# ScalarE's normalization and predicated copies in the opening, and other ends of the edge stages, in one graph-and-experts kernel

## The reference, cut to what matters

```python
x = x + gnn(_layernorm(x), stack([src, dst]), ...)      # L = 2 layers
x = x + experts(_layernorm(x)[None], ...)[0]
# one layer of gnn:
h = x @ w_in + b_in                                     # before the first layer
xn = _layernorm(h, ln1_g[l], ln1_b[l])
q, k, v = xn @ wq[l] + bq[l], xn @ wk[l] + bk[l], xn @ wv[l] + bv[l]   # 8 heads of 32
scores = einsum('ehd,ehd->eh', q[dst], k[src]) * scale  # dst, src: the edges and every node's edge to itself
attn = softmax of scores over the edges of each dst
agg = segment_sum(attn[:, :, None] * v[src], dst)
h = h + agg.reshape(n, 256) @ wo[l] + bo[l]
h = h + gelu(_layernorm(h, ln2_g[l], ln2_b[l]) @ w1[l] + b1[l]) @ w2[l] + b2[l]
```

## Time and profile before

| | us |
|---|---|
| median of 3 runs | 3311.08 (3309.96 to 3312.67) |
| the profiled execution, device time | 3308.49 |
| its span | 3306.3 |
| opening, to the first edge gather | 0 to 199.5 |
| edges(0), first to last gather issue | 199.5 to 1306.2 |
| tail of edges(0), links, mid | 1306.2 to 1690.4 |
| edges(1), first to last gather issue | 1690.4 to 2790.0 |
| tail of edges(1) to the end | 2790.0 to 3306.3 |

### The profile page before, as it was taken

How to read it: one execution, slowest core, us unless ns; L and a number is a source line. 1 busy time by engine, 2 the same in 40 slices (tenths; PEclk the granted TensorE clock), 3 DMA queues, 4 the chain that set the end, 5 groups by cost and what they waited for, 6 DMA issues and landing times. The chain is left out here.

```text
span 3306.3 us, 28610 instructions
## 1 busy us (share of the span) xinstructions
PE 2235.3 (68%) x7207; PEld 1510.9 (46%) x7207; DVE 2490.4 (75%) x3966; ACT 1320.9 (40%) x3886; POOL 1834.8 (55%) x1938
## 2 busy tenths in 40 slices
PE   6745666656566666699956665666666666699798
PEld 4423443433343343476643333344433433477676
DVE  6788888888888888545448888888888888455233
ACT  2224444445545444211224444554544544222222
POOL 5047777777777776212047777777777775221000
PEclk8866767677777766799976777777677767699899
DMA  5357777777777778323357777777777777332111
GB/s 145 105 169 236 243 243 243 243 243 243 245 246 246 243 243 244 84 62 86 82 162 236 244 243 243 243 245 245 246 246 243 244 243 234 78 79 55 45 32 39
DMA packets 249750, 623.51 MB, mean 189 GB/s; under 512 B 50258, under 2 KB 105777, under 8 KB 249592
## 3 DMA queue, kind: packets, MB, share of 16 engines
q0 software_dynamic: 149904, 471.38, 47.9%
q1 hardware_dynamic: 99688, 150.30, 14.6%
HBM read 526.66 MB, written 94.78 MB: 188 GB/s over the span
## 5 line engine op out<-in xcount | busy, mean ns | idle before, releaser
L811 POOL DMA_INDIRECT ring<-kv_table,stage_ix x1760 | 1672.7, 950 | 601.6 <-issue 539.7
L1078 PE MATMUL bank<-ring,hot_w 128*128 128x272 f32 x1760 | 709.9, 543 | 516.9 <-DVE ring L2026 467.3
L1065 PE MATMUL bank<-qs,hot_q 128*128 x1760 | 691.5, 535 | 358.4 <-DVE ring L2003 295.6
L1078 PEld LDWEIGHTS bank<-ring,hot_w 128*128 128x128 f32 x1760 | 418.1, 259 | 790.9 <-DVE ring L2026 630.6
L2003 DVE TENSOR_TENSOR ring<-ring,bank 128x1024 f32<-128x1024 f32 x440 | 533.7, 1213 | 282.0 <-DMA ring<-kv_table,stage_ix 254.9
L1065 PEld LDWEIGHTS bank<-qs,hot_q 128*128 128x128 f32 x1760 | 444.6, 263 | 513.0 <-issue 423.9
L2008 DVE TENSOR_REDUCE s<-ring 128x32 f32<-128x1024 f32 x440 | 533.9, 1213 | 4.2
L1293 ACT ACTIVATE hot_q<-pos_b,row_of 128x128 f32<-128x128 bf16 x880 | 301.0, 392 | 25.2 <-DVEq L1991 16.5
L2020 DVE TENSOR_TENSOR bank<-ring,bank 128x512 f32<-128x512 f32 x440 | 301.8, 686 | 0.0
L2017 DVE TENSOR_TENSOR ring<-ring,bank 128x512 f32<-128x512 f32 x440 | 297.7, 677 | 0.0
L2026 DVE TENSOR_TENSOR ring<-ring,bank 128x512 f32<-128x512 f32 x440 | 295.9, 673 | 0.4
(11 more groups left out here) (333 smaller groups left out, 2214.8 us busy)
## 6 DMA issues: line engine op xcount, KB each, us to landing
agg_d<-stage_o SPq DMA_DIRECT2D x108, 544.0 KB, 4.4
ring<-kv_table,stage_ix POOLq DMA_INDIRECT x1760, 3.8
pos_b<-rel_d SPq DMA_DIRECT2D x54, 256.0 KB, 5.4
kv_table<-ring SPq DMA_DIRECT2D x50, 224.0 KB
h_dram<-ring SPq DMA_DIRECT2D x15, 560.0 KB
ring<-h_dram SPq DMA_DIRECT2D x15, 560.0 KB
ring<-in_x_dram SPq DMA_DIRECT2D x10, 560.0 KB
ring<-kv_table SPq DMA_DIRECT2D x10, 560.0 KB
```

Of the source, the lines that this page charges most:

```text
L811: gps.indirect_dma_start(out=chunk[:, par * G + i, j, :], out_offset=None, in_=table, in_offset=bass.IndirectOffsetOnAxis(ap=stage_ix[:, p ...
L1065: mm = ten.matmul(q_bank(third, i)[:, 0:QC], hot_q[:, i % 4, a * P:(a + 1) * P], qs[:, bass.ds(t * QC + a * QC, QC)], start=(a == 0), stop ...
L1078: mm = ten.matmul(b_acc[i % 2][:, lo - OWN:MC], hot_w[:, i % 4, :], chunk[:, s, j, lo:ROW], start=(j == 0), stop=(j == QD // 2 - 1), skip_ ...
```

## The change

The change moves the opening's norms to ScalarE (GpSimd adds -mean * rstd), does `expand` with a copy and two predicated copies, moves `constants` ahead, weighs ten blocks per layer in one product of 128x1024 with GpSimd adding the pairs, holds SP's weight loads until the last gather has landed, moves parts of `fold` into `links`, does the first batch of mid and last tile by tile, and turns every `hold` but those whose increment is read into a plain wait.

```diff
@@ SyncE
-                        hold(sp, s["done"], ...)
+                        sp.wait_ge(s["done"], ...)
                     if nn == LASTG:
+                        sp.wait_ge(gath[(NB - 1) % SLOTS], (layer + 1) * uses((NB - 1) % SLOTS) * QD * 16)
                         next_weights()
@@ GpSimd, opening: root
                     gps.tensor_scalar(r[:, :], m[:, :, 1], EPS, 1.0, ALU.add, ALU.mult).then_inc(s["rs_step"], 1)
+                    gps.tensor_scalar(f[:, :], m[:, :, 0], -1.0, 0.0, ALU.mult, ALU.add).then_inc(s["rs_step"], 1)
...
+                    gps.tensor_tensor(f[:, :], f[:, :], r[:, :], ALU.mult).then_inc(s["rs_ready"], 1)
@@ GpSimd, homes: one semaphore per tile in the first batch
-                                               in_offset=...).then_inc(s["home"], 16)
+                                               in_offset=...).then_inc(s["home"] if it else S[f"first{j}"], 16)
@@ GpSimd, after the gathers of a layer (LATE = 2)
+                def add_pairs(par, i, n):
+                    pool.wait_ge(S["weighed"], n + 1)
+                    val = chunk[:, par * G + i, :, D:ROW]
+                    gps.tensor_tensor(val[:, 0:2], val[:, 0:2], val[:, 2:4], ALU.add).then_inc(S["w_ready"], 1)
...
+                for k in range(NGRP - 2, NGRP):
+                    for i in range(LATE if k == NGRP - 2 else 0, blocks_of(k)):
+                        add_pairs(k % 2, i, layer * NB + k * G + i)
@@ TensorE
-                turn(0)
-                project(0, 0)
+                for j in range(BT + 1):
+                    if j < BT:
+                        turn_tile(0, j)
+                    if j:
+                        project_tile(0, 0, j - 1)
@@ TensorE, links: between the transposes (L1142) and the product (L1147)
+                if layer:
+                    fold_ups("last")
+                else:
+                    fold_rows("mid")
...
             links(0)
-            fold("mid")
+            fold_ups("mid")
...
             links(1)
-            fold("last")
@@ ScalarE, opening
+                def scaled(at, no, src, j0=0, j1=BT):
+                    r, f = ((rs_x, off_x), (rs, off))[no % 2]
+                    act.wait_ge(s["rs_ready"], no + 1)
+                    if at:
+                        act.wait_ge(s["evac"], at)
+                    for j in range(j0, j1):
+                        sca.activation(tok[:, j, :], src[:, j, :], ACT.Identity, bias=f[:, j:j + 1], scale=r[:, j:j + 1]).then_inc(s["tok"], 1)
+                scaled(0, 0, x_in)
                 turned(0)
+                scaled(o.first(1), 2, x_in)
                 for it in range(NBATCH):
                     if it + 1 < NBATCH:
                         turned(o.first(it + 1))
+                    scaled(o.second(it), 2 * it + 1, h_in[it % 2])
                     turned(o.second(it))
                     for j in range(BT):
                         keys(it, j)
                         if it + 1 < NBATCH:
                             query(it, j)
+                        if it + 2 < NBATCH and j >= 2:
+                            scaled(o.first(it + 2), 2 * it + 4, x_in, 2 * j - 4, min(2 * j - 2, BT))
@@ VectorE, expand
-                do(ts(e_bit, e_m, float(n), None, ALU.is_ge))
-                do(vec.scalar_tensor_tensor(out=e_m, in0=e_bit, ...))
-                to, by = e_pack[:, :, n:P, :], e_move[:, :, n:P, :]
-                do(tt(by, e_pack[:, :, 0:P - n, :], to, ALU.subtract))
+                of, to = (e_pack, e_move) if k % 2 == 0 else (e_move, e_pack)
+                st.did(vec.tensor_copy(to, of))
+                do(ts(e_bit, e_m, float(n), None, ALU.is_ge))
+                st.did(vec.scalar_tensor_tensor(out=e_m, in0=e_bit, ...))
                 for a in range(2):
-                    st.did(tt(by[:, a], by[:, a], e_bit[...].to_broadcast(...), ALU.mult))
+                    bit = e_bit[:, a, n:P].bitcast(U32).rearrange("p (e j) -> p e j", j=1).to_broadcast([HB, P - n, QD])
+                    st.did(vec.copy_predicated(to[:, a, n:P, :], bit, of[:, a, 0:P - n, :]))
                 st.sync(v)
-                do(tt(to, to, by, ALU.add))
@@ VectorE, opening: scaled, turn_x and turn_h are gone; constants() before measure_x(1)
                 projected(0)
+                constants()
                 measure_x(1)
...
-                    turn_h(it)
                     projected(it + 1)
...
-                    if it == 0:
-                        constants()
-                    if it + 2 < NBATCH:
-                        turn_x(it + 2)
-                    else:
-                        turn_h(it + 1)
@@ VectorE, edges: the steps of groups 26 and 27
+                def weigh_late(par, i, n):
+                    val = chunk[:, par * G + i, :, D:ROW].rearrange("p j (d h) -> p j d h", h=H)
+                    w = w_of[:, i].rearrange("p j (a h) -> p j a h", a=1)
+                    tt(val, val, w.to_broadcast([P, QD, DH, H]), ALU.mult).then_inc(S["weighed"], 1)
...
+                    if nn == LASTG:
+                        for i in range(LATE):
...
+                        weigh_late(par, LATE, n + LATE)
+                        weigh_late(par, LATE + 1, n + LATE + 1)
+                        scores(1 - par, LASTG - 1, tn, n + (nk + LASTG - 1), third + 1)
+                        sum_scores(1 - par, LASTG - 1, n + (nk + LASTG - 1))
+                        weigh_late(par, LATE + 2, n + LATE + 2)
+                        return
+                    if not nn:
+                        sum_weights()
+                        for i in range(nk):
+                            weigh_late(par, i, n + i)
+                        return
@@ VectorE, mid and last: the first batch, instead of head(0) and projected(0, ...)
+                def first_head(h, st):
+                    hd = Steps(s["head"])
+                    v.wait_ge(s["x_in"], 2 * ROWS)
+                    hd.did(bias(h_n[kind], bias_sq))
+                    v.wait_ge(s["out_free"], 1)
+                    def put(j):
+                        v.wait_ge(s["mm"], j + 1)
+                        tt(h[:, j, :], h_n[kind][:, j, :], bank[4 + j % 3][0:TN, 0:D], ALU.add).then_inc(s["bank_free"], 1)
+                    def stats(j):
+                        v.wait_ge(s["bank_free"], j + 4)
+                        st.did(vec.bn_stats(stat[:, j, :], h[:, j, :]))
+                    for j in range(BT):
+                        v.wait_ge(S[f"first{j}"], (1 if kind == "mid" else 2) * 16)
+                        own, z = home[:, j, 0:H], home[:, j, H:2 * H]
+                        val = home[:, j, 2 * H:MC].rearrange("p (d h) -> p d h", h=H)
+                        den = small[0:TN, j * H:(j + 1) * H]
+                        mine = own_v[:, j, :].rearrange("p (d h) -> p d h", h=H)
+                        hd.did(tt(den, z, own, ALU.add))
+                        hd.did(tt(mine, mine, own.rearrange("p (a h) -> p a h", a=1).to_broadcast([TN, DH, H]), ALU.mult)); hd.sync(v)
+                        hd.did(ts(den, den, 1e-30, None, ALU.max))
+                        hd.did(tt(mine, mine, val, ALU.add)); hd.sync(v)
+                        hd.did(vec.reciprocal(den, den)); hd.sync(v)
+                        tt(tok[:, j, :].rearrange("p (h d) -> p d h", h=H), mine, den.rearrange("p (a h) -> p a h", a=1).to_broadcast([TN, DH, H]), ALU.mult).then_inc(s["tok"], 1)
+                        if j >= 2:
+                            put(j - 2)
+                            if j >= 3:
+                                stats(j - 3)
+                    assert hd.n == HEAD0, hd.n
+                    put(BT - 2)
+                    stats(BT - 3)
+                    put(BT - 1)
+                    stats(BT - 2)
+                    stats(BT - 1)
+                    st.sync(v)
+                    aggregate()
```

More of the change, by code:

```diff
@@ L68 @@
 LANES = P - G * H
+LATE = 2
+assert LASTG == LATE + 2 and LATE + 3 == G - 3
+HEAD0 = 5 * BT + 1
 QSPACE = 7700
@@ L535, in batch @@
                 def batch(it, last):
-                    hold(sp, s["done"], it + 1, S["sp_passed"])
+                    sp.wait_ge(s["done"], it + 1)
                     tile_rows(rows(out, it), h_b, S["out_done"])
@@ L900, in fold, with fold_ups @@
                             mm = ten.matmul(b[0:TN, 0:c1 - c0], g_col[:, 1, a:a + 1].to_broadcast([P, TN]), w_qkv[:, a, c0:c1], start=(a == 0), stop=(a == 1))
-                if kind in ("mid", "last"):
-                    for f in range(FFN // P):
-                        for a in range(2):
-                            mm = ten.matmul(bank[6][:, f:f + 1], w_up[:, a, f * P:(f + 1) * P], g_col[:, 3, a:a + 1], start=(a == 0), stop=(a == 1))
+                    mm.then_inc(S["w_pe"], 1)
+            def fold_ups(kind):
+                pe.wait_ge(S["w_in_dma"], 16 * W_TOTAL[kind])
+                for f in range(FFN // P):
+                    for a in range(2):
```

(20 more changed lines are left out.)

133 lines of the change are left out of this document (67 added, 66 removed).

## The result

The changed kernel took 3266.97 us (median of 4 runs, 3265.53 to 3270.23), the kernel before 3311.07 beside it: a ratio of 0.9869, 95% interval 0.9853 to 0.9885. The prediction was 3269, so the total was right; several of its terms were not, and their errors largely cancel. The profiled span went from 3306.3 to 3264.3 us, 42.0 less.

| stretch | before | after | change | predicted |
|---|---|---|---|---|
| opening, to the first edge gather | 199.5 | 181.1 | -18.4 | -20 |
| edges(0), first to last gather issue | 1106.7 | 1106.6 | -0.1 | 0 |
| tail 0: last gather issue to the first instruction of links | 32.9 | 25.3 | -7.6 | -7.0 |
| links 0: from there to the first home gather | 19.2 | 17.2 | -1.9 | 0 |
| first batch of mid: from there to its first aggregate | 24.6 | 19.6 | -5.0 | -6 |

The account below looks back on a forecast made before the run. GpSimd's issue of gathers was taken to bound both edge stages; opening -20, tails -7.0 and -3.6, links +2.3, first batches -12 sum to -40.3 us, giving 3268 against the profile, 3271 against the median; predicted 3269, range 3254 to 3287.

Parts of the forecast that it names:

- Opening, norms, -10: Opening: ten sets of five scalings leave VectorE for ScalarE; their worth, read at three places, is -7, -1.7 and -1.3 us.
- the first, -7: Opening: the last node row issues at 72.2 instead of 76.55, so `rows_of_nodes` starts at 76.4 instead of 83.36: -7 us.
- The second place, -1.7: Opening: the set of scalings behind the tables of `rows_of_nodes` leaves VectorE: -1.7 us.
- The third, -1.3: Opening: the next x set leaves VectorE, which then waits for TensorE's queries: -1.3 us (0 to -3).
- The two sets after that I cost at nothing: Opening: two later sets of scalings give 0, as TensorE's keys pace VectorE; without that cover, 3.4 us more.
- Expand, -10: Opening, seven expands: difference and sum go, a copy comes, predicated copies cost what the products did: -10 us (-14 to +1.6).
- SP's new wait removes that: Tail of layer 0: VectorE's 3.40 us wait for the last gather, beside weight loads, goes; with the tail's -3.6: -7.0 us.
- Links 1, +2.3: Links, layer 1: 32 products (6.83 us) go ahead of L1147 in a 4.58 us gap, ending at 2832.07 instead of 2829.82.
- B: Rival, tails: GpSimd's adds pace them, at 2.1 us each; 4 us lost per layer, total 3277; chance 0.12.
- D: Rival, opening's expand: the predicated copy is no stream; 14 copies at 5 us each cost 61, total 3330; chance 0.04.
- E: Rival, whole kernel: the change shifts work without moving the ends; total within 0.2% of now; chance 0.04.
- A: Rival, opening: TensorE and ScalarE pace it; of 20 us only 9 remain, total 3280; chance 0.16.

Follow-up runs that it names:

- run 1: The changed kernel with the old expand (difference, masked product, sum) put back: 3273.34 us.
- run 3: The changed kernel without SP's wait for the last gather ahead of the weight loads: 3267.41 us.
- run 6: The changed kernel with the 32 narrow products of fold (fold_ups) behind the product of links in layer 1, as before: 3264.03 us.
- run 2: The kernel before with the new expand alone: 3300.02 us.
- run 11: The kernel before with every hold whose increment nobody reads as a plain wait, nothing else: 3304.70 us.
- run 4: The changed kernel with the ten adds of a layer back on VectorE, each behind its product: 3279.10 us.
- run 5: The changed kernel with the old first batch of mid and last (five tiles at once): 3276.02 us.
- run 12: The changed kernel with TensorE's opening reordered, node rows earlier, fold_ups behind links' product, three wide products ahead, each layer's last add on VectorE: median 3258.99 us.
- run 10: The changed kernel with fold_ups behind the product of links in layer 1 and three unread wide products in the gap ahead: 3264.67 us.

## Why the prediction was right, and which of its steps were not

- **The bound** was read rightly: the gathers' pace stayed, and every gain ahead of them moved what follows one to one. That the total came within 2 us is in part luck: by the table, the stretches miss by 4.0 us in all on one side and by 5.5 on the other.
- **Opening, norms, -10:** measured -10.2 at the first own score of batch 3 (147.63 before, 137.46 now), but by other steps. Of the prediction's three places the first, -7, gave 3.4 (83.36 to 79.99). "The first run of node rows, which does not move" failed: it started at 34.81 instead of 30.67, since the root of the second x batch ahead of it came later (31.92 instead of 29.00). Ahead of that root stand `projected(0)`, whose first tile came at 19.64 instead of 16.85, and `constants`, which was costed at nothing and now ends at 29.6, 2.9 us after VectorE had begun that batch before. The tile is late because ScalarE's scalings begin 1.2 us later than VectorE's did (12.99 and 11.82), behind GpSimd's longer root, and its evictions of the transposes stand behind all five of them (first at 15.46 instead of 13.05). The second place, -1.7, gave 1.6. The third, -1.3, gave 3.1 (from `projected(3)` to the next own score). "The two sets after that I cost at nothing" failed too: they gave 2.0 (2.8 up to `projected(4)`, 139.53 before and 128.57 now, of which 0.8 are lost again). Too much by 3.6 and too little by 3.8: the -10 is right by luck.
- **Expand, -10:** 11.9 in itself, since a copy took 0.70 and a pair of predicated copies 1.35 (taken: 0.72 and 1.28), and waits between its steps went too; net 8.3 by run 1 and 8.1 by the two traces, because "they are late next" of TensorE was right and worth 3.6 to 3.9 us, which the sum left out. The whole opening gave 18.4 in the profiled run; by the spread of the other runs it is 14 to 19.
- **Tails:** -7.6 and -5.3 where -7.0 and -3.6 were predicted. VectorE's part was right (its last product ends 9.3 and 6.9 us earlier by the last gather's issue; predicted 10.2 and 6.8). The lag behind it was too dear: 1.2 for the add and 2 for lags were taken, 1.66 was measured (3.43 us from the last product's end to links, 1.77 before), because TensorE did a block in 1.1 us, not 1.86, as it had already done in the last blocks before. A gap on ScalarE for a store of `agg_d`, a sign of being wrong, was there (1.15 us), but the last block waited for GpSimd's last add, which ended at 1311.2. "SP's new wait removes that" failed as a step: by run 3 the 3.40 us went without the wait as well, since VectorE now asks later; whether the loads caused them before stays open.
- **Links 1, +2.3:** the mechanism was right, the term mis-sized: 4.5 by run 6, while the holds' end gives some of it back. Of the 4.5, 3.0 are the held product (its gap was 3.2 to 3.8 us in runs 2, 6 and 11, not 4.58) and 1.5 the longer scatters, a term that the prediction did not have.
- **Links 0, 0:** -1.9. Of it 0.63 is the hold ahead of the home gathers; TensorE at its full level takes 1.9 off the product, of which VectorE's wait for it shows 1.2 (0.79 instead of 1.95).
- **First batches, -6 each:** -5.0 and -5.9. In mid the first home gather's issue took 2.48 us instead of 1.24 because of VectorE's addition beside it (last section), which the prediction put at nothing.
- **Holds, 0:** failed. Where nothing covers them they cost: 0.63 at each first home gather and some 1.5 in mid by run 11.
- **Rivals.** B fell by run 4 and the 1.27 us of one add, D by the 0.70 and 1.35 above, E by runs 1 and 5. A was half there: TensorE and then ScalarE do pace the opening's end, and cost some 3 to 4 us of the sum, not 11.

## What to carry to other kernels

When one engine's work in a serial opening is shortened, put a price on the engine that is late next, not only a warning: here it kept 3 to 4 us, and taking that away only showed the one behind it. Filler work moved into a gap must be shorter than the gap at the clock that the engine will have there. An operation moved into an engine's idle time can stretch what another engine does there: VectorE's addition of 1.49 us cost about 1 us of GpSimd's DMA issues in each layer. And a sum that comes out right can stand on two wrong steps: only landmarks between them, compared in both traces, show it.

## What the runs showed of the hardware that was not expected

**A scan that waits for GpSimd.** VectorE's second scan (L2127) took 1.28 us in the tail, and 0.41 in run 4, where GpSimd adds nothing; it ended 0.3 us after GpSimd's pair of adds (1299.95 + 2.53). Both its inputs lie in SBUF; the first scan and the late products, with one input in a PSUM bank, kept their 0.40 and 1.2 us beside the adds. The other way round, GpSimd's small power operation took 4.46 us beside a VectorE product of two SBUF operands, against 1.17 in most others, and the root for which ScalarE waited 8.35 us came 3.3 us later for it:

```profile
82.69 4.46 POOL L738 TENSOR_TENSOR rs_x<-rs_x,half 125x5 f32<-125x5 f32 x1
...
82.65 3.48 DVE L1529 TENSOR_TENSOR ring<-ring,qs 125x3200 f32<-125x3200 f32 x1
```

The Trainium skill says so of the two engines (GPSIMD Engine Reference, section 1): they share their SBUF interfaces, and get in each other's way where a VectorE instruction has two SBUF inputs. The trace agrees, and shows that two inputs are not the only case: a GpSimd product of 125x5 took 1.85 us instead of 0.20 beside VectorE's cast of one SBUF tensor (L740 at 80.02, L1527 at 79.99 for 1.83). The sharing would also explain why the adds paid here, the products beside them reading their weights from PSUM; no run moved the weights.

**GpSimd's DMA issues stretch in the same way.** Beside VectorE's addition of 125x1280, both operands in SBUF, an indirect DMA's issue lasted longer by the time that the two overlapped, less 0.12 or 0.13 us: overlaps of 1.36, 1.21, 1.10, 1.09 and 0.75 us (the first home gather of mid and the second scatter of links 1 in the changed kernel, the first home gather of mid in runs 6 and 12, the second in run 4) made them 1.24, 1.08, 0.98, 0.97 and 0.63 longer. Where the addition stood elsewhere, as in run 5, the same issues took 1.00 and 1.24 us.

**TensorE's clock moves the first gather by some 2.8 us** from run to run with the same program. From the end of TensorE's 6 us pause to the transposes of expand's result it took 25.1 us in the changed kernel and 25.2 in run 6, but 27.8 and 28.0 in runs 4 and 10, granted 0.50 from 164 to 168 us where the others had 1.00. Those two have the late first gathers (184.8 and 185.2; the others 180.6 to 182.4); the last 1 us of their delay arose ahead of that pause. What decides between the levels there is not shown. In links, behind narrow products as behind a pause, the product took 3.95 and 3.97 us; behind wide ones 2.00 to 2.31.
